# Pairwise attention pooling on TensorE: a loop body of one block instead of two, with x as a tenant of the ring of PSUM slots

## What is computed

```python
B, F, D = x.shape                        # 2048, 39, 64
row, col = np.triu_indices(F, k=1)       # 741 pairs
ip = x[:, row, :] * x[:, col, :]
hidden = jax.nn.relu(jnp.einsum('bpd,da->bpa', ip, W_w) + b_w)
logits = jnp.einsum('bpa,a->bp', hidden, W_h) + b_h[0]
a = jax.nn.softmax(logits, axis=1)[:, :, None]
pooled = jnp.sum(a * ip, axis=1)
return pooled @ W_p + b_p
```

## Time and profile before

| | |
|---|---|
| median of 3 runs | 1325.57 us (1322.91 to 1327.94) |
| the profiled execution: its time | 1334.73 us |
| its span, first to last instruction | 1332.9 us |
| mean granted TensorE clock over the span | 0.951 |
| TensorE matmul busy | 1156.1 us, 87% |
| ScalarE busy | 951.3 us, 71% |
| VectorE busy | 934.6 us, 70% |
| GpSimd busy | 286.6 us, 22% |

### The profile page before, as it was taken

How to read it: one execution, slowest core, us unless ns; L and a number is a source line. 1 busy time by engine, 2 the same in 40 slices (tenths; PEclk the granted TensorE clock), 3 DMA queues, 4 the chain that set the end, 5 groups by cost and what they waited for, 6 DMA issues and landing times.

```text
span 1332.9 us, 60251 instructions
## 1 busy us (share of the span) xinstructions
PE 1156.1 (87%) x25856; PEld 517.9 (39%) x25856; DVE 934.6 (70%) x484; ACT 951.3 (71%) x1123; POOL 286.6 (22%) x263
## 2 busy tenths in 40 slices
PE   7988979789787997979979889797997979979984
PEld 3433434334343443434433344333443434434432
DVE  8686667866678675876867767577686776867870
ACT  5776767767677686767857678576785767857873
POOL 3131221212122131221302213032130221312220
PEclk9998989999899998989989899898998989989998
DMA  3142132312423123241222412324122241412312
GB/s 51 30 46 34 28 41 35 47 28 28 41 39 40 31 31 39 39 48 22 33 36 39 49 21 32 37 39 49 21 37 34 37 49 21 48 30 33 46 20 22
DMA packets 333436, 47.63 MB, mean 36 GB/s; under 512 B 333280, under 2 KB 333280, under 8 KB 333280
## 3 DMA queue, kind: packets, MB, share of 16 engines
q1 hardware_dynamic: 331264, 45.16, 26.6%
q10 hardware_dynamic: 2016, 0.01, 0.1%
HBM read 26.59 MB, written 18.54 MB: 34 GB/s over the span
## 4 chain that ended last, share of the span: by engine, by line
PE 85%; issue 12%; ACT 1%; DMA 1%; SPq 1%; ACTq 0%; DVE 0%; DVEq 0%
PE z L481 52%; PE logits L501 25%; PE z L452 4%; PE x_cols L439 3%; ACT hidden L356 1%; PE logits L491 1%; DMA values<-gram 0%; DMA gram<-gram_out 0%; DMA bp_col<-in_L_rec_b_p_dram 0%; SPq L188 0%; ACTq L398 0%; SPq L176 0%; SPq L174 0%; ACTq L392 0%; ACTq L393 0%
## 5 line engine op out<-in xcount | busy, mean ns | idle before, releaser
L356 ACT ACTIVATE hidden<-z,b_col 128x988 f32<-128x988 f32 x768 | 815.1, 1083 | 319.2 <-PE z L481 308.2
L277 DVE TENSOR_TENSOR prod<-x_wide 128x2964 f32<-128x2964 f32 (+1 forms) x257 | 821.7, 3242 | 96.7 <-PE z L481 89.1
L481 PE MATMUL z<-prod,w_tiles 64*32 64x494 f32 x12288 | 833.9, 590 | 4.6 <-ACT hidden L356 2.8
L501 PE MATMUL logits<-hidden,head_w 64*32 64x371 f32 (+1 forms) x8192 | 489.6, 491 | 33.9 <-issue 33.4
L236 POOL COPY head_w<-head_cols 128x64 f32<-128x64 f32 x252 | 277.0, 1099 | 1007.8 <-PE logits L501 1004.6
L481 PEld LDWEIGHTS z<-prod,w_tiles 64*32 64x32 f32 x12288 | 234.0, 108 | 325.6 <-issue 254.1
L501 PEld LDWEIGHTS logits<-hidden,head_w 64*32 64x32 f32 x8192 | 197.7, 109 | 279.3 <-issue 271.8
L259 DVE COPY x_wide<-x_cols 128x624 f32<-128x624 f32 (+1 forms) x64 | 51.4, 804 | 246.1 <-PE x_cols L439 244.1
L340 ACT ACTIVATE x_scaled<-x_wide,wp_col 128x156 f32<-128x156 f32 x256 | 105.9, 414 | 1.2 <-DMA bp_col<-in_L_rec_b_p_dram 1.2
L491 PE MATMUL logits<-w_tiles 64*32 64x2 f32 x256 | 8.3, 185 | 96.3 <-issue 96.3
L452 PE MATMUL z<-x_wide,x_scaled 64*39 64x39 f32 x4096 | 56.5, 202 | 20.6 <-issue 20.6
(11 more groups left out here) (16 smaller groups left out, 14.6 us busy)
## 6 DMA issues: line engine op xcount, KB each, us to landing
x_rows<-in_r_x_dram SPq DMA_DIRECT2D x128, 156.0 KB
gram<-gram_out SPq DMA_DIRECT2D x256, 47.5 KB
gram<-gram_out SPq DMA_DIRECT2D x256, 23.2 KB
values<-gram SPq DMA_DIRECT2D x128, 46.3 KB, 3.6
w_tiles<-in_L_rec_W_w_dram SPq DMA_DIRECT2D x4, 16.0 KB, 2.5
head_cols<-in_L_rec_W_h_dram ACTq DMA_DIRECT2D x4, 0.2 KB, 3.8
out_dram<-y_all SPq DMA_DIRECT2D x4, 1.0 KB, 3.4
out_dram<-y_all ACTq DMA_DIRECT2D x4, 1.0 KB, 4.3
```

What stands on the lines that cost most here:

```text
L277: nc.vector.tensor_tensor(out, one, other, ALU.mult).then_inc(ready, 1)
L356: nc.scalar.activation(hidden[:, i, :, CHUNK * k:CHUNK * (k + 1)], z[:, (slot + item(j)) % 2, :, 0:CHUNK], ACT.Relu, bias=b_col[:, 0:1]).t ...
L481: last = nc.tensor.matmul(z[col:col + TILE, at, b, 0:CHUNK], w_tiles[row:row + D, col:col + TILE], prod[row:row + D, i, first:first + CHUN ...
L501: last = nc.tensor.matmul(logits[TILE * q:TILE * (q + 1), part, 0:cols], head_w[row:row + A, e, b, :], hidden[row:row + A, e, b, first:fir ...
```

## The change

TensorE's loop body becomes one block, and its inner loop four passes; of the last group, the first two blocks are a loop and the last two are written out. For this no slot may depend on the block's parity. The ring `z` gets a third slot, from the banks of `x_cols`, and the transposed x becomes an item of the ring: it takes slot 2 between chunk 3 and chunk 9, and the Gram matrices take slot 1 between chunks 4 and 7. The slots follow a fixed table per block, and each item waits for the one before it in its slot. `x_rows` and `x_wide` get one place each: SyncE loads a block of x once the block before has been transposed, and VectorE spreads it once all products and the Gram matrices of the block before are done. ScalarE scales x in two instructions a block instead of four. At the start, both tiles of the first x are loaded first, and the loads of the head weights and of two scalars go from ScalarE's queue to SyncE's, where the scalars have a semaphore of their own.

```diff
+    SLOT = (2, 1, 0, 2, 1, 0, 0, 1, 0, 2, 1, 0)
+    EARLIER = (9, 10, 11, 0, 1, 2, 5, "gram", 6, "x", 7, 8)
+    X_SLOT, GRAM_SLOT, FIRST_X_SLOT = 2, 1, 0
+    BEFORE_X, BEFORE_GRAM = 3, 4
...
-        x_rows = sb("x_rows", [ROWS, SLOTS, 2 * ROW_DUOS, D])
-        x_wide = sb("x_wide", [P, SLOTS, BLOCK_DUOS, WIDE])
+        x_rows = sb("x_rows", [ROWS, 2 * ROW_DUOS, D])
+        x_wide = sb("x_wide", [P, BLOCK_DUOS, WIDE])
...
-        z = ps("z", [P, 2, 2, BANK])
+        z = ps("z", [P, 3, 2, BANK])
         logits = ps("logits", [P, 2, BANK])
-        x_cols = ps("x_cols", [P, 2, BANK])
...
-            def load(v, slot):
+            def load(v):
+                sp.wait_ge(x_cols_ready, v + 1)
                 for u in range(2):
...
-                        sp.wait_ge(x_cols_ready, v + 2)
-                        load(v + 2, m % SLOTS)
+                        load(v + 2)
...
-                if not (isinstance(v, int) and v < SLOTS):
-                    dve.wait_ge(prod_ready, BLOCK_STEPS * (v - 1))
+                if not first:
+                    dve.wait_ge(prod_ready, BLOCK_STEPS * v)
+                    dve.wait_ge(z_ready, ITEMS * (v - 1) + CROSS_AT + 1)
                 dve.wait_ge(x_cols_ready, 1 if first else v + 2)
...
-            def scale_x(v, slot, i):
+            def scale_x(v, u):
...
-                    if j == 1 and not (isinstance(v, int) and v == 0):
-                        scale_x(v, slot, 3)
-                    if more and j in (6, 7, 10):
-                        scale_x(v + 1, 1 - slot, (6, 7, 10).index(j))
+                    if more and j in (7, 10):
+                        scale_x(v + 1, (7, 10).index(j))
...
-            def cross_work(v, slot, loads=None):
+            def cross_work(v, with_x=True):
 
-                if loads is not None:
-                    pe.wait_ge(x_spread, 2 * (v + 1))
-                    pe.wait_ge(x_loaded[1 - slot], 32 * loads)
+                if with_x:
+                    pe.wait_ge(x_loaded, 32 * (v + 1))
+                    pe.wait_ge(z_read, ITEMS * v + item(BEFORE_X) + 1)
                     nc.tensor.sem_inc(z_claimed, 1)
-                    transpose(1 - slot, range(2))
-                gram_matrices(v, slot)
+                    transpose(X_SLOT, range(2))
+                gram_matrices(v)
...
+            def claim_slot(v, j, with_x):
+
+                earlier = EARLIER[j]
+                if earlier == "gram":
+                    pe.wait_ge(z_read, ITEMS * v + CROSS_AT + 1)
+                elif earlier == "x":
+                    if with_x:
+                        pe.wait_ge(x_spread, 2 * (v + 2))
+                elif earlier < j:
+                    pe.wait_ge(z_read, ITEMS * v + item(earlier) + 1)
+                elif not (isinstance(v, int) and v == 0):
+                    pe.wait_ge(z_read, ITEMS * (v - 1) + item(earlier) + 1)
...
-            def two_blocks(n):
-                block_work(2 * n, 0, n + 1)
-                block_work(2 * n + 1, 1, n + 2)
-
...
-                with pe.Fori(0, GROUP_BLOCKS // 2) as w:
-                    two_blocks(GROUP_BLOCKS // 2 * g + w)
+                with pe.Fori(0, GROUP_BLOCKS) as m:
+                    block_work(GROUP_BLOCKS * g + m)
...
-            two_blocks(BLOCKS // 2 - 2)
-            block_work(BLOCKS - 2, 0)
-            block_work(BLOCKS - 1, 1, following=False)
+            with pe.Fori(BLOCKS - GROUP_BLOCKS, BLOCKS - 2) as v:
+                block_work(v)
+            block_work(BLOCKS - 2, with_x=False)
+            block_work(BLOCKS - 1, following=False)
```

More of the change, by code:

```diff
@@ L126, in bass_pairwise_attention_pooling @@
         first_x_loaded = [sem(f"first_x_loaded{i}") for i in range(2)]
-        x_loaded = [sem(f"x_loaded{i}") for i in range(SLOTS)]
+        x_loaded = sem("x_loaded")
         x_cols_ready = sem("x_cols_ready")
@@ L189, in load_values @@
                             "p (i k) -> p i k", k=OFFSETS), bands).then_inc(values_loaded[slot], 16)
-            sp.dma_start(x_rows[0:FIELDS, 0, :, :], x_rows_dram[0, :, 0, :, :]).then_inc(first_x_loaded[0], 16)
+            for u in range(2):
+                sp.dma_start(x_rows[u * D:u * D + FIELDS, :, :],
+                             x_rows_dram[u, :, 0, :, :]).then_inc(first_x_loaded[u], 16)
             for h in range(2):
@@ L194, in _ @@
                     sp.dma_start(w_tiles[h * D:(h + 1) * D, c * A:(c + 1) * A], w_hidden).then_inc(w_loaded, 16)
-            sp.dma_start(x_rows[D:D + FIELDS, 0, :, :], x_rows_dram[1, :, 0, :, :]).then_inc(first_x_loaded[1], 16)
-            load(1, 1)
+            sp.wait_ge(zeroed, 1)
+            for h in range(2):
+                for b in range(2):
+                    at = GROUP_STEPS - 1 + GROUP_STEPS * (h ^ b)
+                    sp.dma_start(head_cols[h * D:(h + 1) * D, b, at:at + 1],
+                                 w_logit.rearrange("(a o) -> a o", o=1)).then_inc(head_cols_loaded, 16)
+            for col, scalar in ((bh_col, b_logit), (bp_col, b_out)):
+                sp.dma_start(col[:, :],
+                             scalar.rearrange("(a o) -> a o", o=1).broadcast_to((P, 1))).then_inc(scalars_loaded, 16)
+            load(1)
             def group(g, pairs, last=False):
@@ L297, in pool_group, with block_work @@
                                         ALU.mult, ALU.add).then_inc(y_ready, 1)
-            def block_work(v, slot, pooled_group=None, ended=None, more=True):
-                multiply(v, slot, 0)
+            def block_work(v, pooled_group=None, ended=None, more=True):
+                multiply(v, 0)
                 if pooled_group is not None:
@@ L304, in block_work @@
                 for i in range(1, BLOCK_STEPS):
-                    multiply(v, slot, i)
+                    multiply(v, i)
                 if ended is not None:
@@ L355, in rectify @@
                 act.wait_ge(z_ready, ITEMS * v + item(j) + 1)
[L356 to L357 removed]
+                nc.scalar.activation(hidden[:, i, :, CHUNK * k:CHUNK * (k + 1)], z[:, SLOT[j], :, 0:CHUNK],
                                      ACT.Relu, bias=b_col[:, 0:1]).then_inc(z_read, 1)
@@ L375, in exponentials, with block_work @@
                                      accum_out=exp_sum[:, :]).then_inc(logits_free, 1)
-            def block_work(v, slot, writes, ended=None, more=True):
+            def block_work(v, slot, writes, ended=None, more=True, first=False):
                 for j in range(CHUNKS):
-                    rectify(v, slot, j)
+                    rectify(v, j)
+                    if first and j == 1:
+                        scale_x(0, 1)
                     if j == CROSS_AT - 1:
@@ L472, in hidden_layer @@
                     pe.wait_ge(prod_ready, BLOCK_STEPS * v + i + 1)
-                if not (isinstance(v, int) and v == 0 and j < 2):
-                    pe.wait_ge(z_read, ITEMS * v + item(j) - 1)
+                claim_slot(v, j, with_x)
                 nc.tensor.sem_inc(z_claimed, 1)
-                at = (slot + item(j)) % 2
                 for a in range(0, A, TILE):
```

141 lines of the change are left out of this document (63 added, 78 removed).

## The result

The changed kernel takes 1102.05 us (median of 4 runs, 1101.76 to 1104.79) against 1326.76 us for the kernel before in the same session. The ratio is 0.831, with an interval of 0.829 to 0.834. The forecast was 1128 us, in the range 1095 to 1195. Direction and mechanism were right; the time came out 26 us lower.

What follows compares the result with a forecast made beforehand. TensorE was taken to bound the kernel, with stops for code fetched each outer pass. 16.0 + 71.7 + 959.0 + 55.5 + 28.6 = 1130.8 us of span, 1132.6 with 1.8 outside, less half of 9.2: 1128 us, range 1095 to 1195.

Steps and rivals of the forecast that it cites:

- Reading the stops as fetches: TensorE's outer loop: code is fetched anew each pass; the two stops at a group's start cost 6.85 us.
- A: Rival, group's start: the outer branch still misses, stops and slow clock stay, 9.3 us a group, 1259 us; 7%.
- Rival C: Inner loop: its branch back misses in every block, 372 us on top, 1500 us, slower than before; 4%.
- D: Rival, outer loop: stops belong to its wait and branch, whatever the body's size, and stay; about 1310 us; 2%.
- B: Rival: the ring with x binds, by VectorE's late spread or ScalarE's backlog; about 1 us more a block, 1191 us; 8%.
- the third slot: Ring for TensorE's chunks: removes at most 0.7 us a block, 44 us over 63 blocks; taken as 0 in the sum.
- Rival E: TensorE's block: the third slot pays, block falls toward 16.3 us, down to 1084 us; within the likeliest case's 79%.
- The branch's 0.11 us: Inner loop's branch back: 17.00 us with a branch against 16.89 without; 17.0 taken for every block inside the loop.
- The last group: T(60) to T(63), Gram matrices of block 60 to 63: new code again, 18.5 + 17.0 + 20.0 = 55.5 us.
- x in the ring: Chunk 9 waits for VectorE's spread in slot 2: slack 2.4 us, cost 0.
- The start: Up to block 0's Gram matrices, T(0): gains between 0 and 3 us, taken as 16.0 against 17.70.
- Half of the 9.2 us: Runs' median lies 9.2 us below the profiled execution; half taken off 1132.6 us for stops that go away, giving 1128.

Runs made afterwards that it cites:

- the two kernels without stops named above: The changed kernel, 1102.05 us, and the changed kernel with the start's loads in the old order and on the old queues, 1101.73 us.

## Why the prediction was right, and where it was off

| term of the sum | predicted | measured |
|---|---|---|
| T(0) | 16.0 | 15.93 |
| T(0) to T(4) | 71.7 | 69.57 |
| T(4) to T(60), 14 groups | 959.0 (68.5 each) | 937.07 (66.93 each) |
| T(60) to T(63) | 55.5 | 49.54 |
| T(63) to the end of the span | 28.6 | 27.8 |
| span | 1130.8 | 1099.9 |

**Reading the stops as fetches** was right: no packets of code and no stops in the loop, the clock at 1.00, and with the code of two blocks all three are back. Rivals A, C and D fell with it, and B with the blocks at 16.55 us. Rival C stood beside the Trainium skill's rule (page "Runtime: NRT & Kernel Launch", section "Instruction fetch mechanics") of a window of two pages. A body of 800 loads and matmuls branches back 45 times here, and the outer loop 14 times, with no issue stop of over 0.4 us from 40 to 1000 us, so the measurement decides against the rule for TensorE. Against the same section's room of 2048 instructions the runs show less that can be used: 1440 loads and matmuls stay and 1632 don't; the waits and register work are in the code too, and no row here counts them.

**The step that was mis-sized is the third slot**, taken at 0 in the sum with the reason that the difference "recurs with every chunk that opens a step, waited for or not". Three of the four chunks that open a step (9, 0 and 3) are the second of a pair. Each such pair took 1.76 us before and takes 1.66 now, and with the waits of two slots it is long again; so those chunks did wait. That is some 0.3 of the 0.45 us by which a block was overestimated. The fourth, chunk 6 behind the Gram matrices, takes 1.06 us in both kernels in place of 0.83, and is nearly all that a block of 16.55 still has over its work of 16.29. The other 0.11 us is the branch back, which isn't seen any more. The waits of two slots with a branch in each block give 17.01 us, which is the 17.0 of the forecast; the sum thus priced a ring of two slots. Over the 14 groups that is 22 of the 31 us by which the span was overestimated (1.57 a group, of it 1.35 in three ordinary blocks). Rival E, held to be possible inside the range, is what came, at about 28 of its 44 us.

**The branch's 0.11 us was read from the wrong block.** The body branches back between blocks 4g + 1 and 4g + 2, so T(3) to T(4) has no branch in it; its excess is a pair of chunks of 1.88 us (at 84.22). The block that has the branch, T(2) = 59.47 to T(3), happens to take 17.00 too, and shows it in the logit half right behind it:

```profile
61.30 0.72 PE logits L501 x16
```

So the price was right by luck.

**The last group** was put at 55.5 us from the stops of before, and took 49.5 (17.03, 16.58 and 15.93): its new code is fetched (7 packets from 1000 to 1076 us) without a long stop until T(63), and the last of the three blocks has no transposes in it (0.62 us). The third slot isn't needed for that: with the waits of two slots the same three take 50.8. With two blocks in the loop and those waits they take 53.2, and 58.3 before. What makes the difference stays open.

**x in the ring** cost nothing, as forecast, and the slack was real. But the tightest place isn't chunk 9, it is the group's maximum. **The start** came out at 15.93 us where 16.0 was put, in one execution, and the order of the loads doesn't show in the time. **Half of the 9.2 us** between the profiled execution and the median was taken off. In the changed kernel that gap is 0.3 us. I read from this that all of it had belonged to the stops, though one profiled execution of each kernel doesn't show it. Then nothing should have been taken off a sum that has no stops: the forecast would have been 1132.6 us, and the 4.6 brought it nearer by luck.

## What to carry to other kernels

Look at the code queue before looking for a better schedule: if it moves packets in each pass of an outer loop, the whole of that loop's code must shrink until it stays, and on this TensorE the room was between 1440 and 1632 loads and matmuls. Making buffers independent of parity is worth some slack elsewhere if it halves the code. When a period has a small excess over its work that recurs at regular places, ask which buffer's release falls there, and try other waits before calling it the engine's own.

## What was unexpected of the hardware

- A loop just over the room is fetched whole in each pass (9 packets a group), not only by its excess, and four blocks written out cost only about 1% more than two.
- The kernel before had medians of 1313 to 1327 us in five sessions, and the two kernels without stops named above differ by 0.3 between two of them. It looks as if the stops differ with the session; no run tests it.
- The granted clock fell to 0.50 where TensorE hadn't paused: behind 20 openings in a row, and within the alternation of transposes and logit matmuls.
- Alternating transposes with matmuls of narrow tiles took 7.4 us for work that takes 1.24 in two runs.
